# ScalarE's move of the transposed tile ahead of the slot's exponential, and three steps a third of a slot later

## The chip, the cores and the metric

The kernel runs on one core of a Trainium2 chip. The metric is the device time of one execution in microseconds. Engines are called PE (TensorE, matrix multiplication), DVE (VectorE), ACT (ScalarE), POOL (GpSimd) and SP (SyncE, which only issues DMAs here).

## What is computed

Eight sequences (B) of 512 rows (S) of 256 numbers (D) go through an adapter with a layer norm, and then through an attention block with a feed-forward part:

```python
# adapter: down to 64, exact gelu, one of 16 experts, up to 256, residual, layer norm
hidden = gelu(x @ down_W.T + down_b);  hidden = hidden @ Wsel.T + bsel + domain_emb
x = layernorm(hidden @ up_W.T + up_b + x) * ln_gamma + ln_beta
# attention block, 16 heads of 16
scale, shift = split(silu(sin_emb(timestep)) @ W_ada + b_ada)
x = ln(x) * (1 + scale) + shift
q, k, v = x @ Wq + bq, x @ Wk + bk, x @ Wv + bv
scores = q @ k.T / 4 + attention_bias;  scores[mask] = -inf      # (8, 16, 512, 512)
x = x + (softmax(scores) @ v) @ Wo + bo
h = ln(x) * g2 + beta2
out = x + gelu2(h @ W1 + b1) @ W2 + b2                            # gelu2(x) = x * sigmoid(1.702 x)
```

The attention bias is a tensor of its own for every head, 128 MB in all.

## The kernel before

The 4096 rows are cut into 16 chunks (`NCH`) of 256 rows. One iteration `i` of the main loop does the attention of chunk `i`: 16 heads times 2 blocks of 128 query rows are 32 slots (`TI`). The loop is unrolled into five instruction streams, one for each engine. Each engine works strictly in its own written order; semaphores alone tie them together.

In slot `t` of iteration `i` the engines do this for one tile of 128 queries by 512 keys:

- PE: `score(t)` (L805), one matmul of q and k, both split into bf16 parts, into bank `sc[t % 2]`. It waits for the maximum of slot t-2, which reads that bank.
- POOL: once for two slots, the mask is subtracted from the bias tile of a head (L489).
- DVE: `find_max(t)` (L1337) adds the bias to the scores, writes the sum over the bias tile and keeps a row value `mx`.
- ACT: `soften(t)` (L951), the exponential in place, with the row sums.
- PE: `turn(n)` (L812), four transposes of the exponentiated tile of four slots earlier (`LAG = 4`, `n = 32 i + t - 4`), into bank `tp[n % 2]`. It waits for exponential n and for the move of tile n-2.
- ACT or DVE: `move(n)` copies that bank to `pT` in SBUF. ACT has 21 of the 32 tiles (L957), DVE the 11 of `DVE_MOVES` (L1344), counted by tile. In the slots 12, 14, 15, 17, 19, 21, 24, 27 to 29 and 31, DVE moves.
- PE: `weigh` (L771), twice for each group of eight tiles, multiplies `pT` with the values.

So "move 9" below is the move that stands in slot 9, and "turn 11" the turn of slot 11.

Between these stand all the other steps: each has a time written out in a table, as slot plus 0, 0.3 or 0.6. `each_slot` runs the steps of `t.0`, then the first of two given actions, then the steps of `t.3`, the second action, and the steps of `t.6`. On PE the first is the score and the second the turn; on DVE the maximum and the move; on ACT, before, the exponential and the move. Within one time, the steps of the norm and of q, k, v come first, then the feed-forward's, then the output projection's.

The steps that matter here, for the chunk `a = i + 2` that is being prepared: the adapter's up matmul (PE 0.3), DVE's norms (1.6 to 10.6; the last, `shift`, writes `xm`, L1088), PE's `turn_rows` of xm at 12.6 (L555), ACT's copy of the result to `xT1` at 14.0 (L842), PE's `keys` (L581) at 15.3 and 16.0, which wait for this copy and for DVE's last part of q, and the splitting of k into three bf16 parts by turns: ACT 16.6, DVE 17.3, ACT 17.6, DVE 18.6, with the store by SP at 19.6. q of the next chunk is projected at 8.6 and 10.0 and split by ACT at 11.0 and 12.3 and by DVE at 11.6 and 13.0.

The feed-forward of chunk `i - 2` has eight up-projections `w1` (each a bias matmul L715 and two projections L717, of 128x256 outputs) in four pairs; each pair goes through ACT's `tanh` and DVE's `gate` (L1296), and a new pair waits until the gate has freed its bank. The eight `w2` steps (L734) are the down-projection. In odd iterations the next adapter down matmul runs at 24.3 and 25.3 and its gelu on ACT at 26.6, with a table load before and after it. The last three chunks have tables of their own in `ffn_at` and `mid_at`.

Of the kernel before, what the change touches and what calls it, by code (L numbers as in the profile page):

```python
# [29 lines left out]
LAG = 4  # L30
# [10 lines left out]

PE_AT = dict(up=0.3, v=(1.0, 2.0), q=(8.6, 10.0), xt1=12.6, k=(15.3, 16.0), down=(24.3, 25.3),
             pv=((14.0, 15.0), (22.0, 23.0), (30.0, 31.0), (6.0, 7.0)), spread=(23.3, 7.3))
ACT_AT = dict(q=(11.0, 12.3), widen=(18.3, 2.3), spread=(24.6, 8.0), k=(16.6, 17.6), xT1=14.0, gelu=26.6)
DVE_AT = dict(x1=1.6, st0=2.3, mv0=2.6, v=3.0, n1=4.0, n2=6.3, st1=7.0, mv1=7.6, m1=8.3, m2=10.6, q=(11.6, 13.0),
              k=(17.3, 18.6), recip=(17.6, 1.6), ctx=(25.3, 9.3))
SP_AT = dict(tail=1.0, x=3.0, q=13.6, stack=(17.0, 19.0, 26.0), mask=12.0, mod=12.3, xt=27.0, k=19.6,
             keys=(20.3, 22.0, 27.0))  # L50
POOL_AT = dict(rs0=6, rs1=8, xs=10, mask=16, rs2=16)
MID = dict(wo=(21.0, 21.6), x2=22.6, copy=23.0, st2=23.6, mv2=24.3, hn=27.0, ht=28.6)
FFN = dict(hT=30.0, w1=(3.0, 4.0, 8.0, 9.0, 12.3, 13.0, 17.0, 18.0), tanh=(5.0, 9.6, 14.3, 19.0),
           gate=(6.0, 10.3, 15.3, 19.6), w2=(19.0, 20.0, 23.6, 24.6, 25.6, 26.0, 27.0, 28.0), out=29.6, store=31.0)
GATE = 1.702 / 2
LAST = NCH
# [25 lines left out]
def ffn_at(f):  # L82

    at, i = dict(FFN, hT=FFN["hT"] - TI), f + 2
    if f == NCH - 3:
# [21 lines left out]
def wait(eng, sem, value):  # L107

    if value <= 0:
        return  # L110
    eng.wait_ge(sem, value)
# [7 lines left out]
def on_act(n):  # L119

    return n % TI not in DVE_MOVES
# [7 lines left out]
def head_of(hh):  # L129

    return 8 * (hh // 8) + 2 * (hh % GH) + hh // GH % 2
# [8 lines left out]
def each_slot(i, t, steps, first, second):  # L140

    steps(float(t), round(float(TI * i + t), 1))
    first()
    steps(round(t + 0.3, 1), round(TI * i + t + 0.3, 1))
    second()
    steps(round(t + 0.6, 1), round(TI * i + t + 0.6, 1))


def build(nc, x, x_t, t_tok, e_tok, bias, mask, downT, upT, up_b, experts, gamma, beta,
# [16 lines left out]
    with ExitStack() as ctx:  # L166
        def sb(name, shape, dt=F32):
            return ctx.enter_context(nc.sbuf_tensor(name, shape, dt))
# [42 lines left out]
        xT1 = [sb(f"xT1{n}", [P, CT, CH]) for n in range(2)]  # L211
# [20 lines left out]
        hT = sb("hT", [P, CT, CH])  # L232
# [318 lines left out]
        def _(pe):  # L551
# [117 lines left out]
            def body(i, attn, prev, nxt, pre, qv, down):  # L669
                a, c = i + 2, i + 1  # L670
                AT = PE_AT

# [158 lines left out]
        def _(act):  # L831
# [13 lines left out]
            def queries(c, part):  # L845
                if part == 0:
                    act.wait_ge(s["p_q"], c + 1)
                    wait(act, s["q_out"], 32 * c)
                    for mt in range(2):
                        cols = slice(mt * CH, (mt + 1) * CH)  # L850
                        last = act.activation(qb[:, 0, cols], q_bank(c)[:, cols], ACT.Identity, bias=nbq[:, mt:mt + 1])
                    last.then_inc(s["a_q0"], 1)
                else:
                    act.wait_ge(s["d_qr"], c + 1)
                    act.copy(qb[:, 1, :], q_bank(c)[:, :]).then_inc(s["a_q1"], 1)

            def keys(c, part):
                if part == 0:
                    act.wait_ge(s["p_k"], c + 1)
                    wait(act, s["k_out"], 64 * (c - 1))  # L860
                    for mt in range(2):
                        cols = slice(mt * CH, (mt + 1) * CH)
                        last = act.activation(kb[c % 2][:, 0, cols], k_bank(c)[:, cols], ACT.Identity,
                                              bias=vec[:, VEC["bk"] + mt:VEC["bk"] + mt + 1])
                    last.then_inc(s["a_k0"], 1)
                else:
                    act.wait_ge(s["d_kr"], c + 1)
                    act.copy(kb[c % 2][:, 1, :], k_bank(c)[:, :]).then_inc(s["a_k1"], 1)
# [20 lines left out]
            def body(i, attn, prev, nxt, pre, qv, down):  # L889
                a, c = i + 2, i + 1  # L890
                AT = ACT_AT

                def norm_steps(t):
                    if qv and t in AT["q"]:
                        queries(c, AT["q"].index(t))
                    if pre and t in AT["k"]:
                        keys(a, AT["k"].index(t))
                    if pre and t == AT["xT1"]:
                        copy_rows(a)
                    if down and t == AT["gelu"]:  # L900
                        adapter_gelu((i + 3) // 2)

                def ffn_steps(f, at):
                    when = ffn_at(f)
                    if at == when["hT"]:
                        act.wait_ge(s["p_ht"], f + 1)
                        wait(act, s["p_w1"], 4 * f)
                        for ct in range(CT):
                            last = act.activation(hT[:, ct, :], lb[:, ct * CH:(ct + 1) * CH], ACT.Identity,
                                                  scale=vec[:, VEC["g2"] + ct:VEC["g2"] + ct + 1],  # L910
                                                  bias=vec[:, VEC["beta2"] + ct:VEC["beta2"] + ct + 1])
                        last.then_inc(s["a_hT"], 1)
                    if at in when["tanh"]:
                        p = when["tanh"].index(at)
                        act.wait_ge(s["p_w1"], 4 * f + p + 1)
                        wait(act, s["d_act"], 4 * f + p - (1 if f == NCH - 1 else 0))
                        act.activation(tanh_of(f, p), w1_bank(f, p)[:, :], ACT.Tanh, scale=GATE  # L917
                                       ).then_inc(s["a_th"], 1)

                def mid_steps(m, at):  # L920
                    if at == mid_at(m)["copy"]:
                        act.wait_ge(s["d_x2"], m + 1)
                        wait(act, s["d_out"], m - 1)
                        act.copy(x2s[m % 2][:, :], lb[:, :]).then_inc(s["a_x2"], 1)

                def steps(t, at):
                    norm_steps(t)
                    for f in range(max(0, i - 2), min(i, NCH)):
                        ffn_steps(f, at)
                    if i > 0:  # L930
                        mid_steps(i - 1, at)
                    for r in range(2):
                        if (prev if r else attn) and t == AT["widen"][r]:
                            ri = 2 * (i - r) + r
                            act.wait_ge(s["d_recip"], ri + 1)
                            wait(act, s["p_rin"], ri)
                            act.copy(rwide[:, :, :].rearrange("p j (h d) -> p j h d", d=HD),
                                     rinv[:, :, :].unsqueeze(3).to_broadcast([P, 2, 8, HD])).then_inc(s["a_wide"], 1)
                        if (prev if r else attn) and t == (4.3 if i == NCH else AT["spread"][r]):
                            ri = 2 * (i - r) + r  # L940
                            act.wait_ge(s["p_rin"], ri + 1)
                            wait(act, s["d_ctx"], ri)
                            act.copy(rin[:, :], inverse_bank(ri)[:, CH:2 * CH]).then_inc(s["a_rin"], 1)

                def soften(t):
                    hh, j = t // 2, t % 2
                    act.wait_ge(s["smax"], TI * i + t + 1)
                    if t % (TI // 2) == 0:
                        wait(act, s["d_recip"], 2 * (i - 1) + t // (TI // 2) + 1)
                    tile = bias_s[:, (H * i + hh) % NB, j, :]  # L950
                    act.activation(tile, tile, ACT.Exp, bias=mx[:, t:t + 1], scale=-1.0,  # L951
                                   accum_out=sums[:, j, head_of(hh):head_of(hh) + 1]).then_inc(s["probs"], 1)

                def move(n):
                    act.wait_ge(s["pt_ready"], n + 1)
                    wait(act, s["pv_done"], n // TG - 1)
                    act.copy(pT[n // TG % 2][:, n // 2 % GH, :, (n % 2) * P:(n % 2 + 1) * P],  # L957
                             tp[n % 2][:, :].rearrange("p (k q) -> p k q", k=KT)).then_inc(s["copied_a"], 1)

                for t in range(TI):  # L960
                    n = TI * i + t - LAG
                    each_slot(i, t, steps, lambda: soften(t) if attn else None,
                              lambda: move(n) if (attn if t >= LAG else prev) and on_act(n) else None)

            each_iteration(body)

# [449 lines left out]
```

## Time and profile before

| | |
|---|---|
| median of 3 runs | 1038.88 us (1038.23 to 1039.96) |
| profiled execution | 1044.28 us, span 1042.4 us |
| granted clock of PE, mean of the span | 0.966 |
| busy, share of the span | PE 90%, DVE 69%, ACT 68%, POOL 66% |
| DMA | 207 MB, mean 199 GB/s |

The profile is of one execution. Busy time of PE counts matmuls whose ends are modelled and which overlap, so two matmuls may be shown over the same moment. In the timeline each line is an instruction, or several of one kind in a row (x4), with its start and duration in us, and in brackets how long the engine had been idle and what released it.

### The profile page before, as it was taken

To read this page: it belongs to the slowest core of one execution; us is meant where nothing else is said; L and a number is where in the kernel's file an instruction comes from. 1 tells how busy PE (TensorE), PEld (TensorE's weight loads), DVE (VectorE), ACT (ScalarE), POOL (GpSimd) and SP (SyncE) were. 2 spreads that over 40 slices of the span, in tenths; PEclk is the share of its full clock that TensorE was granted. 3 is DMA by queue.
4 is the path that set the end of the run, shared out by engine and by line. 5 is a ranking of instruction groups with operands and counts; after the bars stand their busy time and mean duration, and the time that the engine had idled before them with its cause. 6 is when DMAs were issued, how large, how long until landed. Compare 5 with 4: busy or idle time off the path is not lost.

```text
span 1042.4 us, 20949 instructions
## 1 busy us (share of the span) xinstructions
PE 935.6 (90%) x6621; PEld 663.3 (64%) x6621; DVE 720.7 (69%) x1911; ACT 707.6 (68%) x1675; POOL 685.7 (66%) x391
## 2 busy tenths in 40 slices
PE   3566888999999999999999999999999999999987
PEld 1444555676667766676667766676667767676665
DVE  5836766777777777777777777777777777674542
ACT  2225777777777777777777777777777777777541
POOL 2437786867677776867677676877677776784600
PEclk8678898999999999999999999999999999999998
DMA  5399758776796758765796659776796659665200
GB/s 159 91 263 296 240 187 234 222 212 192 227 275 181 212 182 245 220 212 193 225 275 184 209 182 236 228 213 193 218 261 187 196 178 264 206 199 151 90 11 11
DMA packets 147950, 207.42 MB, mean 199 GB/s; under 512 B 14385, under 2 KB 62322, under 8 KB 147842
## 3 DMA queue, kind: packets, MB, share of 16 engines
q1 hardware_dynamic: 147842, 206.09, 66.8%
q8 instruction: 55, 0.90, 0.4%
q14 instruction: 53, 0.43, 0.1%
HBM read 185.05 MB, written 20.99 MB: 198 GB/s over the span
## 4 chain that ended last, share of the span: by engine, by line
PE 51%; issue 16%; DVE 13%; ACT 11%; POOL 6%; DMA 1%; SPq 0%; DVEq 0%; ACTq 0%; POOLq 0%
PE tp L812 12%; PE pv L771 8%; PE la L734 7%; PE sc L805 6%; PE lc L717 6%; POOL bias_s L489 5%; DVE bias_s L1337 4%; PE lb L581 4%; ACT bias_s L951 3%; ACT pT L957 3%; PE lb L751 3%; DMA bias_s<-in_bias 1%; DVE st L1076 1%; DVE xm L1088 1%; PE lb L597 1%
## 5 line engine op out<-in xcount | busy, mean ns | idle before, releaser
L489 POOL TENSOR_TENSOR bias_s<-mask_f,bias_s 128x1024 f32<-128x1024 f32 x256 | 603.4, 2371 | 228.6 <-DMA bias_s<-in_bias 228.1
L951 ACT ACTIVATE bias_s<-bias_s,mx 128x512 f32<-128x512 f32 x512 | 369.9, 723 | 263.3 <-DVE mx L1337 259.4
L1337 DVE CUSTOM_DVE_ANT_0 bias_s<-sc,bias_s 128x512 f32<-128x512 f32 x512 | 348.5, 685 | 197.2 <-PE sc L805 182.6
L812 PE MATMUL tp<-ident,bias_s 128*128 128x128 f32 x2048 | 314.7, 277 | 41.9 <-ACT pT L957 38.4
L812 PEld LDWEIGHTS tp<-ident,bias_s 128*128 128x128 f32 x2048 | 251.6, 143 | 140.8 <-ACT bias_s L951 67.5
L805 PE MATMUL sc<-stk,stq 128*128 128x512 bf16 x512 | 198.0, 387 | 11.5 <-DVE mx L1337 9.4
L957 ACT COPY pT<-tp 128x512 f32<-128x512 f32 x336 | 191.1, 569 | 0.5 <-PE tp L812 0.5
L771 PE MATMUL pv<-pT,v_all 128*32 128x256 f32 x2048 | 138.7, 389 | 0.5 <-issue 0.5
L734 PE MATMUL la<-w_s,act_s 128*128 128x256 f32 x512 | 128.3, 380 | 1.0 <-DVE act_s L1296 1.0
L1344 DVE COPY pT<-tp 128x512 f32<-128x512 f32 x176 | 120.5, 685 | 7.9 <-PE tp L812 7.8
L717 PE MATMUL lc<-hT,w_s 128*128 128x256 f32 x464 | 122.0, 386 | 0.0
L805 PEld LDWEIGHTS sc<-stk,stq 128*128 128x128 bf16 x512 | 50.1, 98 | 74.5 <-DVE mx L1337 34.0
L951 ACT ACTIVATION_READ_ACCUMULATOR bias_s<-bias_s,mx 128x1 f32 x512 | 97.0, 190 | 0.0
L734 PEld LDWEIGHTS la<-w_s,act_s 128*128 128x128 f32 x512 | 89.2, 190 | 9.7 <-DVE act_s L1296 1.3
L717 PEld LDWEIGHTS lc<-hT,w_s 128*128 128x128 f32 x464 | 81.0, 195 | 9.5 <-issue 0.3
L771 PEld LDWEIGHTS pv<-pT,v_all 128*32 128x32 f32 x2048 | 54.1, 110 | 47.9 <-issue 25.8
L499 POOL TENSOR_SCALAR rs<-mv 128x2 f32<-128x2 f32 x48 | 9.3, 193 | 84.7 <-DVE mv L1083 82.5
L1296 DVE SCALAR_TENSOR_TENSOR act_s<-th,lc 128x512 f32<-128x512 f32 x57 | 39.2, 687 | 35.8 <-ACT th L917 35.7
L1337 DVE DVE_READ_ACCUMULATOR2_ANT mx<- 128x1 f32 x512 | 42.7, 83 | 0.0
L581 PE MATMUL lb<-xT,wk_s 128*128 128x256 f32 x120 | 34.0, 410 | 8.9 <-ACT xT L842 8.9
L715 PE MATMUL lc<-b1sel,b1p 128*128 128x256 bf16 x116 | 32.3, 278 | 7.7 <-DVE act_s L1296 4.3
L500 POOL TENSOR_TENSOR rs<-rs,powc 128x2 f32<-128x2 f32 x48 | 33.5, 698 | 4.0
(188 smaller groups left out, 848.4 us busy)
## 6 DMA issues: line engine op xcount, KB each, us to landing
bias_s<-in_bias SPq DMA_DIRECT2D x256, 512.0 KB, 4.2
stq<-q_parts SPq DMA_DIRECT2D x128, 96.0 KB, 3.7
stk<-k_parts SPq DMA_DIRECT2D x128, 96.0 KB, 4.0
k_parts<-kb SPq DMA_DIRECT2D x32, 192.0 KB, 2.3
q_parts<-qb SPq DMA_DIRECT2D x32, 192.0 KB, 2.3
xT<-in_x_t SPq DMA_DIRECT2D x8, 512.0 KB, 5.9
k_parts<-kb SPq DMA_DIRECT2D x32, 128.0 KB, 2.4
stq<-q_parts SPq DMA_DIRECT2D x64, 64.0 KB, 3.8
```

The source lines that it names most:

```text
L489: pool.tensor_tensor(tile, mask_f[:, :, :], tile, ALU.subtract).then_inc(s["masked"], 1)
L581: last = pe.matmul(bank[:, mt * CH:(mt + 1) * CH], w[:, ct, mt * P:(mt + 1) * P], xT1[c % 2][:, ct, :], start=(ct == 0), stop=(ct == CT - 1))
L717: last = pe.matmul(h, w1_s[:, ct, ft * P:(ft + 1) * P], hT[:, ct, :], start=False, stop=(ct == CT - 1))
L734: last = pe.matmul(rows, act_s[:, ft, j * P:(j + 1) * P], w2_s[:, ft, :], start=False, stop=(ft == FT - 1))
L771: last = pe.matmul(pv[32 * h:32 * h + 32, 0:CH], v[:, kt, col:col + 2 * HD], pT[gi % 2][:, h, kt, :], start=(g % 2 == 0 and kt == 0), stop ...
L805: pe.matmul(sc[t % 2][:, :].rearrange("p (e k) -> p e k", e=2), stq[:, hh, j * P:(j + 1) * P], stk[:, :, hh, :], start=True, stop=True).th ...
L812: last = pe.transpose(tp[n % 2][:, kt * P:(kt + 1) * P], bias_s[:, n // 2 % NB, n % 2, kt * P:(kt + 1) * P], ident[:, :])
L951: act.activation(tile, tile, ACT.Exp, bias=mx[:, t:t + 1], scale=-1.0, accum_out=sums[:, j, head_of(hh):head_of(hh) + 1]).then_inc(s["prob ...
L957: act.copy(pT[n // TG % 2][:, n // 2 % GH, :, (n % 2) * P:(n % 2 + 1) * P], tp[n % 2][:, :].rearrange("p (k q) -> p k q", k=KT)).then_inc( ...
L1296: dve.scalar_tensor_tensor(out=act_s[:, 2 * p:2 * p + 2, :].rearrange("p c n -> p (c n)"), in0=tanh_of(f, p), scalar=1.0, in1=w1_bank(f, p ...
L1337: dve.tensor_tensor_reduce(out=tile, in0=sc[t % 2][:, :], in1=tile, scale=1.0, scalar=BIG, op0=ALU.add, op1=ALU.min, accum_out=mx[:, t:t + ...
L1344: dve.tensor_copy(pT[n // TG % 2][:, n // 2 % GH, :, (n % 2) * P:(n % 2 + 1) * P], tp[n % 2][:, :].rearrange("p (k q) -> p k q", k=KT)).th ...
```

## The change

On ACT the move becomes the first action of a slot and the exponential the second. The two key projections go a third of a slot later on PE, ACT's two key parts from 16.6 and 17.6 to 17.0 and 18.0, DVE's first key part from 17.3 to 17.6. Four up-projections (the last two pairs) go a third of a slot or two thirds later. The feed-forwards of the last three chunks (13 to 15) have their own tables and keep them; chunks 0 to 12, in iterations 2 to 14, use the changed one.

```diff
-PE_AT = dict(up=0.3, v=(1.0, 2.0), q=(8.6, 10.0), xt1=12.6, k=(15.3, 16.0), down=(24.3, 25.3),
+PE_AT = dict(up=0.3, v=(1.0, 2.0), q=(8.6, 10.0), xt1=12.6, k=(15.6, 16.3), down=(24.3, 25.3),
...
-ACT_AT = dict(q=(11.0, 12.3), widen=(18.3, 2.3), spread=(24.6, 8.0), k=(16.6, 17.6), xT1=14.0, gelu=26.6)
+ACT_AT = dict(q=(11.0, 12.3), widen=(18.3, 2.3), spread=(24.6, 8.0), k=(17.0, 18.0), xT1=14.0, gelu=26.6)
...
-              k=(17.3, 18.6), recip=(17.6, 1.6), ctx=(25.3, 9.3))
+              k=(17.6, 18.6), recip=(17.6, 1.6), ctx=(25.3, 9.3))
...
-FFN = dict(hT=30.0, w1=(3.0, 4.0, 8.0, 9.0, 12.3, 13.0, 17.0, 18.0), tanh=(5.0, 9.6, 14.3, 19.0),
+FFN = dict(hT=30.0, w1=(3.0, 4.0, 8.0, 9.0, 13.0, 13.6, 17.6, 18.3), tanh=(5.0, 9.6, 14.3, 19.0),
...
-                    each_slot(i, t, steps, lambda: soften(t) if attn else None,
-                              lambda: move(n) if (attn if t >= LAG else prev) and on_act(n) else None)
+                    each_slot(i, t, steps, lambda: move(n) if (attn if t >= LAG else prev) and on_act(n) else None,
+                              lambda: soften(t) if attn else None)
```

## Rows read from the trace of the kernel before

**Rows 1.** The page, busy us, share of the span and instructions
```profile
PE 935.6 (90%) x6621; PEld 663.3 (64%) x6621; DVE 720.7 (69%) x1911; ACT 707.6 (68%) x1675; POOL 685.7 (66%) x391
```

**Rows 2.** Stretches: length; busy of PE, PEld, DVE, ACT, POOL; clock; DMA, GB/s
```profile
120.00:960.00 840.00, 796.31 (x5870) 570.35 (x5868) 611.37 (x1622) 628.93 (x1499) 610.01 (x339) 0.99 0.72 214
```

**Rows 3.** Waits of PE, 120 to 960 us: us in total, times, longest
```profile
PE tp L812 <- ACT pT L957: 29.9, 55, 1.3
PE lb L581 <- ACT xT L842: 7.1, 13, 1.0
```

**Rows 4.** Timeline of PE, iteration 8, slots 10 to 12: start, duration, [idle before]
```profile
552.43 0.38 PE L805 MATMUL sc<-stk,stq 128*128 128x512 bf16 x1
552.65 0.60 PE L812 MATMUL tp<-ident,bias_s 128*128 128x128 f32 x4
553.09 0.38 PE L805 MATMUL sc<-stk,stq 128*128 128x512 bf16 x1
553.63 0.63 PE L812 MATMUL tp<-ident,bias_s 128*128 128x128 f32 x4 [0.17 <-ACT pT L957]
554.10 0.38 PE L805 MATMUL sc<-stk,stq 128*128 128x512 bf16 x1
554.77 0.28 PE L715 MATMUL lc<-b1sel,b1p 128*128 128x256 bf16 x1 [0.29 <-DVE act_s L1296]
...
556.19 0.60 PE L555 MATMUL la<-ident,xm 128*128 128x128 f32 x4
```

**Rows 5.** Timeline of PE, iteration 8, slot 5
```profile
542.22 0.38 PE L805 MATMUL sc<-stk,stq 128*128 128x512 bf16 x1
543.24 0.63 PE L812 MATMUL tp<-ident,bias_s 128*128 128x128 f32 x4 [0.64 <-ACT pT L957]
```

**Rows 6.** Timeline of ACT, iteration 8, slot 9 and the tanh of 9.6
```profile
552.20 0.72 ACT L951 ACTIVATE bias_s<-bias_s,mx 128x512 f32<-128x512 f32 x1 [0.90 <-DVE mx L1337]
...
552.92 0.56 ACT L957 COPY pT<-tp 128x512 f32<-128x512 f32 x1
553.39 0.60 ACT L917 ACTIVATE th<-lc 128x512 f32<-128x512 f32 x1
```

**Rows 7.** Timeline, turns 20 and 31 of iteration 7, turn 0 of 8; exponential 27
```profile
511.36 0.63 PE L812 MATMUL tp<-ident,bias_s 128*128 128x128 f32 x4 [0.53 <-ACT pT L957]
...
531.01 0.73 ACT L951 ACTIVATE bias_s<-bias_s,mx 128x512 f32<-128x512 f32 x1
...
532.99 0.60 PE L812 MATMUL tp<-ident,bias_s 128*128 128x128 f32 x4
...
535.47 0.63 PE L812 MATMUL tp<-ident,bias_s 128*128 128x128 f32 x4 [0.80 <-ACT pT L957]
```

**Rows 8.** Timeline of PE, iteration 7, score 15 and the first keys
```profile
500.89 0.39 PE L805 MATMUL sc<-stk,stq 128*128 128x512 bf16 x1
501.79 1.13 PE L581 MATMUL lb<-xT,wk_s 128*128 128x256 f32 x4 [0.51 <-ACT xT L842]
```

**Rows 9.** Timeline of DVE, iteration 8: maximum 10, gate, xm, maximum 11
```profile
552.99 0.69 DVE L1337 CUSTOM_DVE_ANT_0 bias_s<-sc,bias_s 128x512 f32<-128x512 f32 x1 [0.48 <-PE sc L805]
...
554.02 0.69 DVE L1296 SCALAR_TENSOR_TENSOR act_s<-th,lc 128x512 f32<-128x512 f32 x1 [0.33 <-ACT th L917]
554.62 0.87 DVE L1088 SCALAR_TENSOR_TENSOR xm<-la,rs,mod 128x256 f32<-128x256 f32 x2
555.41 0.68 DVE L1337 CUSTOM_DVE_ANT_0 bias_s<-sc,bias_s 128x512 f32<-128x512 f32 x1
```

**Rows 10.** Waits of PE, 60 to 182 us (iterations 0 and 1)
```profile
PE tp L812 <- ACT pT L957: 15.1, 20, 1.3
...
PE tp L812 <- DVE pT L1344: 2.8, 2, 1.4
...
PE lb L581 <- ACT xT L842: 2.0, 2, 1.0
```

**Rows 11.** Stretches, 160 to 164 us (iteration 1)
```profile
160.00:164.00 4.00, 3.31 (x11) 2.60 (x12) 1.34 (x5) 2.54 (x7) 2.37 (x1) 0.50 0.76 217
```

## The prediction

> **What bounds the kernel now.** I read the page's busy times first, then the table of stretches, then the waits of TensorE (PE), and last the timelines of the slots in which it waits. The page gives PE 90% of the span. In the stretch 120 to 960 us it is busy for 796.3 of 840 us at a granted clock of 0.99, while VectorE (DVE), ScalarE (ACT) and GpSimd (POOL) each have 610 to 629 us [rows 1, 2]. So PE is the bound in the steady part, and what can be won is its own idle time, 43.7 us there. The waits name it: 29.9 us in 55 places before a `turn` (the four transposes of L812) until an ACT move has ended, and 7.1 us before the first key projection until ACT's copy of xT [rows 3]. The rest is mostly the wait for a gate at step 12.3, 0.29 us each time [rows 4]. In the timelines they come back at the same slots in each of the 12 iterations 2 to 13: slot 5 (0.64 us), slot 11 (0.17), slot 20 (0.53), step 15.3 (0.51), and at slot 0 (0.80) after each odd iteration, in which ACT also computes the adapter's gelu [rows 4, 5, 7, 8]. The 55 places are 12 at slot 5, 13 at slot 11, 12 at slot 20, 6 at slot 0, 10 in iteration 1 and 2 in iterations 14 and 15.
>
> **A wait costs more than its idle time.** In slot 10 nothing is waited for, and the turn starts 0.22 us after the score; in slot 11 there is 0.17 us of idle time, and it starts 0.54 us after: 0.32 late. In slot 5, with 0.64 idle, it starts 1.02 after: 0.80 late [rows 4, 5]. The score is shown busy for 0.38 us although its successor normally starts at 0.22, so each wait behind a score costs its idle time plus 0.16, and 0.03 more because the waiting group of four runs less overlapped (0.47 to its successor, against 0.44) [rows 4]. The Trainium skill's "Perfetto Trace Analysis" (section "Tensor Engine Instruction") says that the profiler estimates where a TensorE instruction ends and doesn't observe it; the spacing of starts here agrees. By idle times alone the steady part of the sum below would be 25 us, by starts it is 35, and I take the starts.
>
> **ACT's move ahead of its exponential.** Nothing is added or removed; two instructions of each slot trade places. Turn(t) overwrites the bank that the move of slot t-2 reads. In slot 9 ACT starts its exponential at 552.20, as late as that because it waited 0.90 us for DVE's maximum; the move runs from 552.92 to 553.48, and turn 11 starts at 553.63 [rows 4, 6]. The tile to be moved was there long before, since turn 9 stands a slot's work earlier on PE. Ahead of the exponential, move 9 ends near 552.3, while PE asks for turn 11 at 553.31. I walked the others in the same way: move 3 ends near 541.3 and PE asks at 542.44; move 18 ends 0.9 us before PE asks; move 30, queued behind gelu, three exponentials and the copy to hT, loses one exponential with its accumulator read (0.72, from 552.20 to 552.92) and about 0.3 from slot 26, where the move gets ahead too: it ends just before PE asks. So these waits go: slot 5 (0.64 + 0.19) and slot 20 (0.53 + 0.19) in 12 iterations, 18.6 us; slot 0, 0.99 in five iterations and 1.49 in iteration 2, 6.4 us [rows 5, 7].
> What is queued behind the move now is the exponential, which from here on waits for turn(t) as well as for the maximum. Turn(t+4) is the first to want its result, about 7 us later. The tightest place is the odd iteration, where exponential 27 stands behind gelu and two table loads: it starts at 531.01, is done at 531.74, and turn 31 starts at 532.99 [rows 7]. With 1.2 us left I cost this at nothing; if the cover were gone, it would be the overrun, in 7 iterations.
> ACT's steps at .3 stand between move and exponential as before, but on the other side of each. The tanh of 9.6 starts one move (0.47) earlier [rows 6]; q's second part at 12.3 gets ahead of exponential 12, so that the xT copy at 14.0 comes some 1 us earlier against PE.
>
> **Keys a third of a slot later.** The keys start 0.90 us after the score, 0.68 over the normal 0.22 [rows 8], and their group of four takes 0.09 longer than one without a wait: 0.77 in 12 iterations, 9.3 us, gone by the earlier copy alone; the later step only adds cover. On ACT, 16.6 to 17.0 and 17.6 to 18.0 change no place in the queue. On DVE, 17.3 to 17.6 lets the move of slot 17 go ahead of the keys' remainder; this ends the wait of turn 19 for that move, 1.4 us, in iterations 0 and 1 [rows 10]. SP's store of k at 19.6 follows DVE's part at 18.6, which doesn't move.
>
> **Up-projections: 12.3, 13.0, 17.0, 18.0 to 13.0, 13.6, 17.6, 18.3.** The first no longer waits for the gate of 10.3. But slots 10, 11 and 12 are now bare pairs of score and turn (0.66 us, from 552.43 to 553.09), and behind them at 12.6 comes `turn_rows`, which reads DVE's xm. Without a wait PE is there at 552.43 + 3 x 0.66 = 554.4 [rows 4]. On DVE, maximum 10 starts at 552.99 and frees the engine at 553.60 (its 0.69 less the overlap); the gate, now held by tanh until 554.02, follows at once and takes 0.60, and xm 0.87 more: it is there at 555.1, against 555.5 now [rows 9]. So PE waits 0.7 us at 12.6. The old delays were 0.32 + 0.03 at slot 11 and 0.67 - 0.22 = 0.45 at 12.3, the new one is 0.7: this part gives 0.1 us x 12 = 1 us, and the wait changes its name from gate to xm. The pair moved from 17.0 removes one wait, in iteration 14.
>
> **The ends.** Iterations 0 and 1 have no up-projections, so PE has less to do between its waits: from 60 to 182 us it waited 15.1 us for ACT moves, 2.8 for DVE moves and 2.0 for xT, in 24 places [rows 10]; with 0.19 each, 24.5 us. The largest, at slots 18 to 20, come from exponentials and key parts that stand ahead of moves, and go; but score 20 will then wait for maximum 18, which follows the key part. Bounds: 5 us (these three slots alone, half of it) to 24; I take 15, nearer to the upper since the order causes most of it. Iterations 14 and 15 hold 2 us behind turns and 0.8 behind gates: 2.5 us with the overlaps.
> Sum: 18.6 + 6.4 + 9.3 + 1 + 15 + 2.5 = 52.8 us. The profiled execution took 1044.3 us (span 1042.4) and would take 991.5; the median of the runs is 1038.9, 5.4 lower, and the same saving gives **986 us**. The period of an iteration, now 57.9 or 59.2 us, becomes about 55.6.
>
> **What else is near.** DVE, ACT and POOL, busy 73 to 75% now, go to 79% [rows 2]. The bias tiles' DMAs are issued when turns are done, so they come earlier with them.
>
> **Rivals.** (1) More: the clock falls less often, and xm comes in time. The stretch 160 to 164, right behind the three long waits of iteration 1, ran at 0.50, that is 1.2 GHz [rows 11]. PE's 3.3 us of work in it would take half at the other level; there are three such stretches from 100 us on, all in iterations 0 and 1, so 2 to 6 us, and xm in time 8 more: 972 to 980 us. The Trainium skill's "TensorE: Matmul & The Clock Gate" (section "Part 1: The HAM clock gate") says that lack of activity lowers the clock and activity frees it; the trace agrees, and the rule would add to the gain. Chance 0.15. (2) Half the waits come back under other names: scores that wait for maxima in the bare slots 10 to 12 and 16 to 20, and the ends giving 5: 24 to 34 us in all, 1005 to 1015 us. For it: maximum 11 starts at 555.41, 2.3 us after its score [rows 4, 9]. Against: PE shows no idle time for maxima in the steady part. Chance 0.17. (3) Slower: the ring of turn(t), move(t), exponential(t) and turn(t+4) becomes the pace, because each exponential now starts after a turn. It decides once an exponential lags its score by over four slots, 7 us; it outweighs the gain from 4.4 us per iteration on, and at 5 us gives 1046. Against: the largest lag now, behind gelu, is 4.4 us. Chance 0.04. (4) The change doesn't do what it says: the maximum and not the order holds the move, and all waits stay, 1038 us. Against: in slot 9 the order alone costs 0.72 us [rows 6]. Chance 0.02.
> My own case has 0.62 and reaches from 980 to 1000 us. Measurement can tell 0.2% from no change. Faster 0.94, within 0.2% 0.02, slower 0.04. The range, 974 to 1010, takes in most of rival 1 and half of rival 2.
>
> **What would show it.** Right: L812's idle time until ACT's pT in 120 to 960 us falls from 29.9 to under 5 us; the keys' wait for xT is gone; a new wait of L555 (la, xm) for DVE of about 0.5 us stands once in each of iterations 2 to 13; PE is busy 97% or more. Wrong: L805 waiting for the maximum, or L812 for ACT's exponential, by over 10 us; no wait at L555; a period above 57 us.

## The result

| | before | after |
|---|---|---|
| median of 6 runs | 1039.4 us (1038.2 to 1043.4) | 989.4 us (988.1 to 992.8) |
| profiled execution | 1044.3 us, span 1042.4 | 990.3 us, span 988.4 |
| ratio | | 0.952, 95% interval 0.950 to 0.954 |

The forecast was 986 us with a range from 974 to 1010: 50 us were saved where 52.8 were forecast. The page of the changed kernel: busy time, the chain that ended last, and from the groups of instructions the turn on PE and the move on ACT (busy us, mean ns | idle us before them, what ended it).

```profile
PE 918.3 (93%) x6621; PEld 663.4 (67%) x6621; DVE 715.2 (72%) x1911; ACT 708.5 (72%) x1675; POOL 685.4 (69%) x391
...
PE 80%; issue 7%; POOL 6%; DVE 5%; ACT 1%; DMA 1%; SPq 0%; POOLq 0%; DVEq 0%; ACTq 0%
...
L813 PE MATMUL tp<-ident,bias_s 128*128 128x128 f32 x2048 | 311.7, 275 | 8.1 <-ACT pT L958 4.9
...
L958 ACT COPY pT<-tp 128x512 f32<-128x512 f32 x336 | 195.9, 583 | 101.9 <-PE tp L813 99.5
```

The same work (6621 matmuls) is now 93% of the span, and the chain runs over PE for 80% of it. All lines have moved down by one. The move now waits 99.5 us for its turn: ACT stands ready in front of the tile instead of coming late to it. That idle time costs nothing. On the page of before the same move hardly ever waited (0.5 us in all):

```profile
L957 ACT COPY pT<-tp 128x512 f32<-128x512 f32 x336 | 191.1, 569 | 0.5 <-PE tp L812 0.5
```

The stretch that answers to [rows 2], and the waits of PE in it, which answer to [rows 3]:

```profile
120.00:910.00 790.00, 774.68 (x5797) 565.82 (x5797) 600.71 (x1607) 624.18 (x1485) 604.48 (x336) 1.00 0.76 224
```

```profile
PE sc L806 <- DVE mx L1338: 4.5, 3, 1.9
PE la L556 <- DVE xm L1089: 3.9, 12, 0.3
PE tp L813 <- ACT pT L958: 3.6, 7, 0.8
```

PE is busy 98% there, after 95%. The wait for ACT moves fell from 29.9 us in 55 places to 3.6 in 7, all of them in iterations 1 and 2; the keys' wait for xT is gone, and the new wait for xm stands exactly 12 times, once in each of iterations 2 to 13. The three long waits for a maximum are in iterations 1 and 2 as well. Here is the wait for xm in the timeline of PE, iteration 8, slots 10 to 13, with the same slots of iterations 9 and 10 behind it; this answers to [rows 4]:

```profile
518.53 0.38 PE L806 MATMUL sc<-stk,stq 128*128 128x512 bf16 x1
518.74 0.60 PE L813 MATMUL tp<-ident,bias_s 128*128 128x128 f32 x4
...
519.84 0.39 PE L806 MATMUL sc<-stk,stq 128*128 128x512 bf16 x1
520.27 0.63 PE L813 MATMUL tp<-ident,bias_s 128*128 128x128 f32 x4
521.22 0.66 PE L556 MATMUL la<-ident,xm 128*128 128x128 f32 x4 [0.33 <-DVE xm L1089]
...
522.69 0.38 PE L806 MATMUL sc<-stk,stq 128*128 128x512 bf16 x1
...
575.80 0.65 PE L556 MATMUL la<-ident,xm 128*128 128x128 f32 x4 [0.33 <-DVE xm L1089]
...
632.68 0.66 PE L556 MATMUL la<-ident,xm 128*128 128x128 f32 x4 [0.33 <-DVE xm L1089]
```

From one xm wait to the next are 54.58 and 56.88 us, 111.46 for two iterations. Before, turn 11 of iteration 8 started at 553.63 [rows 4] and that of iteration 10 at the line below, 117.15 us for two.

```profile
670.78 0.63 PE L812 MATMUL tp<-ident,bias_s 128*128 128x128 f32 x4 [0.17 <-ACT pT L957]
```

ACT in slot 9 and the tanh behind it, and DVE from maximum 10 to xm, in the changed kernel; they answer to [rows 6] and [rows 9]:

```profile
517.86 0.59 ACT L958 COPY pT<-tp 128x512 f32<-128x512 f32 x1 [0.60 <-PE tp L813]
518.34 0.72 ACT L952 ACTIVATE bias_s<-bias_s,mx 128x512 f32<-128x512 f32 x1
...
519.06 0.58 ACT L918 ACTIVATE th<-lc 128x512 f32<-128x512 f32 x1
519.54 0.59 ACT L958 COPY pT<-tp 128x512 f32<-128x512 f32 x1
```

```profile
519.08 0.69 DVE L1338 CUSTOM_DVE_ANT_0 bias_s<-sc,bias_s 128x512 f32<-128x512 f32 x1 [0.48 <-PE sc L806]
...
519.70 0.68 DVE L1297 SCALAR_TENSOR_TENSOR act_s<-th,lc 128x512 f32<-128x512 f32 x1
520.30 0.87 DVE L1089 SCALAR_TENSOR_TENSOR xm<-la,rs,mod 128x256 f32<-128x256 f32 x2
```

The move comes ahead of its exponential, the tanh follows both, and the gate no longer waits for the tanh: it starts at once behind the maximum (519.70), and xm is done 2.6 us after score 10 (518.53), where the forecast had 2.7. The next move, that of slot 10, stands behind the tanh and ends at 520.13; turn 12 starts 0.14 us later (520.27).

Last, the move that the prediction had left the least room, the one behind a gelu: move 30 and turn 0 in the timeline of iteration 8, which answers to [rows 7].

```profile
501.54 0.57 ACT L958 COPY pT<-tp 128x512 f32<-128x512 f32 x1
502.42 0.60 PE L813 MATMUL tp<-ident,bias_s 128*128 128x128 f32 x4
```

The move ends at 502.11, and turn 0 starts 0.31 later without a wait. Only turn 12 had less room, and it was held: it starts 0.43 us after its score, where 0.22 is normal.

**Where the 54 us between the two spans went.** I took the start of score 0 of each iteration from both timelines. Iterations 3 to 13, which repeat, are called the steady part from here on. Ahead of the loop 1.4 us were saved, in iteration 0 7.7 (63.7 to 56.0 us), in iteration 1 9.8 (57.9 to 48.1), in iterations 3 to 13 together 30.8, in iteration 14 1.3, and behind it 3.5. Iteration 2 took 0.5 us longer than before (58.4 to 58.9). That one was to save 3.9 us.

### The profile page after: what moved, and what is told of

It is laid out like the page before. It is cut to its first block, busy times and chain, and to the rows that moved or that the text cites. A ratio compares the mean times of both kernels' runs of the same rounds, so it can differ in the third digit from the quotient of the medians.

```text
span 988.4 us, 20949 instructions
## 1 busy us (share of the span) xinstructions
PE 918.3 (93%) x6621; PEld 663.4 (67%) x6621; DVE 715.2 (72%) x1911; ACT 708.5 (72%) x1675; POOL 685.4 (69%) x391
## 4 chain that ended last, share of the span: by engine, by line
PE 80%; issue 7%; POOL 6%; DVE 5%; ACT 1%; DMA 1%; SPq 0%; POOLq 0%; DVEq 0%; ACTq 0%
PE tp L813 19%; PE pv L772 12%; PE la L735 11%; PE sc L806 11%; PE lc L718 10%; POOL bias_s L490 5%; PE lb L582 4%; PE lb L752 3%; PE lb L598 2%; PE lc L716 1%; DVE xm L1089 1%; PE la L572 1%; PE lc L564 1%; PE la L556 1%; PE lb L556 1%
## 5 line engine op out<-in xcount | busy, mean ns | idle before, releaser
L490 POOL TENSOR_TENSOR bias_s<-mask_f,bias_s 128x1024 f32<-128x1024 f32 x256 | 603.1, 2373 | 188.4 <-DMA bias_s<-in_bias 188.1
L958 ACT COPY pT<-tp 128x512 f32<-128x512 f32 x336 | 195.9, 583 | 101.9 <-PE tp L813 99.5
L500 POOL TENSOR_SCALAR rs<-mv 128x2 f32<-128x2 f32 x48 | 9.3, 193 | 78.4 <-DVE mv L1084 76.0
L501 POOL TENSOR_TENSOR rs<-rs,powc 128x2 f32<-128x2 f32 x48 | 33.5, 699 | 4.0
L752 PE MATMUL lb<-wo_s,ctxn 128*128 128x256 f32 x128 | 33.0, 381 | 1.4 <-DVE ctxn L1318 1.4
```

What stands on the lines that cost most here:

```text
L490: pool.tensor_tensor(tile, mask_f[:, :, :], tile, ALU.subtract).then_inc(s["masked"], 1)
L752: last = pe.matmul(lb[:, j * D:(j + 1) * D], ctxn[:, ct, j * P:(j + 1) * P], wo_s[:, ct, :], start=(ct == 0), stop=(ct == CT - 1))
```

## Which part did it

Four kernels, each compared with the kernel before. First only the order on ACT, with the tables of before:

```diff
-                    each_slot(i, t, steps, lambda: soften(t) if attn else None,
-                              lambda: move(n) if (attn if t >= LAG else prev) and on_act(n) else None)
+                    each_slot(i, t, steps, lambda: move(n) if (attn if t >= LAG else prev) and on_act(n) else None,
+                              lambda: soften(t) if attn else None)
```

> Only ACT's order is changed; keys and up-projections keep the times of before. My theory (the order carries the gain; the later up-projections trade the wait for the gate at 12.3 for a slightly longer wait for xm at 12.6): 986 to 989 us, level with the changed kernel or up to 3 us below it. L805 to L812 waits for ACT moves gone as in the changed kernel, no wait at L555 for xm in iterations 2 to 13, a wait of 0.1 to 0.3 us at step 12.3 for the gate instead, no wait of the keys for xT, and turn 19 of iterations 0 and 1 waits about 1 us for DVE's move. Rival (the tables carry part of it): the wait of the keys stays, and with it 5 to 9 us: 995 us or more.

Measured: 985.7 us, ratio 0.948 (0.946 to 0.950). The order alone gives all that the change gives, and 0.4 us per iteration more: in iterations 3 to 13 it has periods (from one score 0 to the next) of 54.18 and 56.49 us by turns, the changed kernel 54.58 and 56.88. Its waits of PE, 120 to 910 us:

```profile
PE lc L716 <- DVE act_s L1297: 4.4, 15, 1.0
...
PE tp L813 <- DVE pT L1345: 2.1, 1, 2.1
```

The wait for the gate at 12.3 is still there, and turn 19's wait for the DVE move is 2.1 us, where I expected 1; it occurs in iterations 0 and 1 only. There the keys also still wait 0.36 us for xT, where I expected nothing; in the steady part they don't.

Then only the tables, with the exponential first and the move second as before (the changed entries alone, abridged from four lines):

```diff
-k=(15.3, 16.0)  k=(16.6, 17.6)  k=(17.3, 18.6)  w1=(..., 12.3, 13.0, 17.0, 18.0)
+k=(15.6, 16.3)  k=(17.0, 18.0)  k=(17.6, 18.6)  w1=(..., 13.0, 13.6, 17.6, 18.3)
```

> Only the tables are changed; ACT keeps the exponential first. My theory: the waits at slots 5, 20 and 0 stay in full, the keys' wait shrinks from 0.51 to about 0.2 us, and in slots 11 to 13 turn 12 now waits for move 10 and step 12.6 for xm, 0.4 us more than before: 1036 to 1041 us, no change that can be measured. Rival (the tables carry part of the gain): 1030 us or less.

Measured: 1025.3 us, ratio 0.986 (0.984 to 0.989). My theory was wrong and its rival right: the tables alone save 14 us. Its waits of PE (120 to 950 us) and turn 12 of iteration 7:

```profile
PE tp L813 <- ACT pT L958: 33.8, 57, 1.3
```

```profile
481.66 0.63 PE L813 MATMUL tp<-ident,bias_s 128*128 128x128 f32 x4 [0.83 <-ACT pT L958]
```

The waits at slots 5, 11 and 0 were there as expected, and turn 12's new wait as well (0.83 us of idle time, 12 times). But the keys' wait and the one at slot 20 were gone in all of iterations 2 to 13. Two more kernels ask which entry does it. The first has the keys' new times alone, the second those of the last up-projection pair alone, and the rest as before (the first edit is abridged from three lines):

```diff
-k=(15.3, 16.0)  k=(16.6, 17.6)  k=(17.3, 18.6)
+k=(15.6, 16.3)  k=(17.0, 18.0)  k=(17.6, 18.6)
 ...
```

> The kernel before with only the keys' times changed (PE 15.6 and 16.3, ACT 17.0 and 18.0, DVE 17.6). With the tables alone the kernel ran in 1025 us, where I expected no change; this and the next run ask which table entry does it. Theory: the keys. DVE's key part behind the move of slot 17 and keys behind turn 15 let maximum 18 start 1.3 us earlier, so move 18 is in time for turn 20 although the exponential stands ahead of it; and half of the keys' wait is covered. The waits at slots 5, 11, 12.3 and 0 stay as before, the period falls from 57.9 and 59.2 to about 56.8 and 58.1 us, and iterations 0 and 1 lose the wait of turn 19: 1018 to 1026 us. Rival (the up-projections from 17.0 and 18.0 do it): 1033 us or more, with the wait at slot 20 as before.

```diff
-w1=(3.0, 4.0, 8.0, 9.0, 12.3, 13.0, 17.0, 18.0)
+w1=(3.0, 4.0, 8.0, 9.0, 12.3, 13.0, 17.6, 18.3)
 ...
```

> The kernel before with only the last pair of up-projections moved, from 17.0 and 18.0 to 17.6 and 18.3. Theory of the keys: score 18 is 1 us earlier, but maximum 18 stands behind DVE's key part, which waits for ACT, so nothing changes at slot 20: 1036 to 1041 us. Rival: the wait of 0.53 us at slot 20 goes and the time is 1030 us or less.

Measured: the keys' times alone 1022.4 us, ratio 0.985 (0.980 to 0.989), period 56.91 and 58.24; the pair alone 1038.1 us, ratio 0.999 (0.996 to 1.001). Waits of PE, first with the keys' times (120 to 945 us), then with the pair (120 to 960 us):

```profile
PE tp L812 <- ACT pT L957: 23.5, 45, 1.3
```

```profile
PE tp L812 <- ACT pT L957: 30.0, 56, 1.3
PE lb L581 <- ACT xT L842: 7.1, 13, 1.0
```

With the keys' times the 12 waits at slot 20 and the keys' own are gone; with the pair both are as in [rows 3]. The keys' table works through DVE. Its first key part waits for ACT, and behind it stand the move of slot 17 and maximum 18. In the timeline of iteration 7 with the keys' times (PE, then DVE, then DVE) score 18, the key part and maximum 18:

```profile
492.18 0.38 PE L805 MATMUL sc<-stk,stq 128*128 128x512 bf16 x1
```

```profile
492.32 0.88 DVE L1164 SCALAR_TENSOR_TENSOR lb<-lb,vec,kb 128x256 f32<-128x256 f32 x2
...
493.26 0.63 DVE L1337 CUSTOM_DVE_ANT_0 bias_s<-sc,bias_s 128x512 f32<-128x512 f32 x1
```

and with the pair alone:

```profile
502.81 0.38 PE L805 MATMUL sc<-stk,stq 128*128 128x512 bf16 x1
...
503.88 0.88 DVE L1164 SCALAR_TENSOR_TENSOR lb<-lb,vec,kb 128x256 f32<-128x256 f32 x2 [1.44 <-ACT kb L863]
...
505.43 0.63 DVE L1337 CUSTOM_DVE_ANT_0 bias_s<-sc,bias_s 128x512 f32<-128x512 f32 x1
```

Maximum 18 starts 1.1 us after its score in the first, 2.6 us in the second. In the kernel before, DVE's key part had waited less:

```profile
507.41 0.88 DVE L1164 SCALAR_TENSOR_TENSOR lb<-lb,vec,kb 128x256 f32<-128x256 f32 x2 [0.47 <-ACT kb L863]
```

The pair brought score 18 forward by a microsecond, and the key part's wait for ACT, which grew from 0.47 to 1.44 us, used it up: counted from score 0, maximum 18 starts at 34.8 us with and without the pair, and at 33.8 with the keys' times. So the wait at slot 20 and the keys' wait each have two cures, the order and the keys' times. Either is enough; together they do not add. The later up-projections cost something besides (3 us between the tables alone and the keys' times alone, 5 us in the next section), so the parts' savings, 53 and 14, come to 50 in the change and not to 67.

## What each table entry is worth once the order is changed

The changed kernel with the up-projections back:

```diff
-w1=(3.0, 4.0, 8.0, 9.0, 13.0, 13.6, 17.6, 18.3)
+w1=(3.0, 4.0, 8.0, 9.0, 12.3, 13.0, 17.0, 18.0)
```

> The changed kernel with the up-projections back at 12.3, 13.0, 17.0 and 18.0. My theory: they are worth less than nothing once the order is changed, since step 12.3 fills the time in which step 12.6 would wait for xm: 984 to 988 us, the period of iterations 3 to 13 shorter by 0.2 to 0.5 us, no wait at L555. Rival (the later up-projections are worth their place): 991 us or more, with a wait at 12.3 longer than the 0.33 us of idle time at L555.

Measured: 984.4 us, ratio 0.947 (0.945 to 0.948), iterations 3 to 13 at 54.18 and 56.49 us, no wait at L556, and 0.21 us for the gate at step 12.3 in each of them. The later up-projections lose 0.4 us per iteration, 5 us in all.

The changed kernel with the keys back:

```diff
-k=(15.6, 16.3)  k=(17.0, 18.0)  k=(17.6, 18.6)
+k=(15.3, 16.0)  k=(16.6, 17.6)  k=(17.3, 18.6)
```

> The changed kernel with the keys back at the times of before. Theory: with the move first, the keys' times matter only in iterations 0 and 1, where turn 19 then waits about 2.1 us for DVE's move of slot 17, as it does with the order alone: iterations 3 to 13 keep 54.6 and 56.9 us, 990 to 994 us. Rival (the keys' times hold part of the steady gain as well): their period grows by 0.5 us or more, 996 us or above.

Measured: 992.3 us, ratio 0.956 (0.951 to 0.960); iterations 3 to 13 unchanged (54.58 and 56.88), and in iterations 0 and 1 turn 19 waits 2.11 us each time. The waits of PE have it once, since their stretch starts at 120 us with iteration 1:

```profile
PE tp L813 <- DVE pT L1345: 3.0, 2, 2.1
```

The 3 us between this kernel and the changed one are not clear of the noise: it ran twice, and its interval overlaps the other's. What is shown is that the keys' times are worth nothing in the steady part once the order is changed.

The two steps at 12.6 and 13.0 changed round:

```diff
-xt1=12.6, ...  w1=(3.0, 4.0, 8.0, 9.0, 13.0, 13.6, 17.6, 18.3)
+xt1=13.0, ...  w1=(3.0, 4.0, 8.0, 9.0, 12.6, 13.6, 17.6, 18.3)
```

> The changed kernel with PE's turn_rows at 13.0 instead of 12.6 and the fifth up-projection at 12.6 instead of 13.0, so that these two trade places. If the 0.33 us of idle time at L555 is a wait for xm that other work can fill: the wait goes, 0.5 us in each of 12 iterations, 982 to 985 us. Rival (it only comes back at the next step, as a wait for the gate or a maximum): 988 to 991 us with the same idle time under another name.

Measured: 983.5 us, ratio 0.946 (0.944 to 0.948), 6 us less than the changed kernel. The period is 54.03 and 56.33, 0.55 shorter, and PE is busy for 605.4 of the 605.8 us of iterations 3 to 13. The xm wait was one that other work can fill.

## Is the exponential off the path

One more instruction on ACT right behind each exponential, in both orders, to a tile that nobody reads (four spare tiles of 128x128 in turn, and a semaphore of their own for the reuse), so that the computation is unchanged:

```diff
                     act.activation(tile, tile, ACT.Exp, bias=mx[:, t:t + 1], scale=-1.0, ...)
+                    wait(act, s["spared"], TI * i + t - 3)
+                    act.copy(spare[t % 4][:, :], ident[:, :]).then_inc(s["spared"], 1)
```

> The kernel before with one more ACT instruction right behind each exponential, a copy of 128x128 into a tile that nobody reads, 0.2 to 0.3 us. Theory (with the exponential first, it lies on the way from the maximum to the move and from there to PE's turn): each wait for a move grows by the copy or more, 1 us or more per iteration, 1052 to 1065 us, and L812's idle time until ACT's pT grows by 10 us or more. Rival (ACT has 30% idle time, so its length doesn't count): under 1043 us.

> The changed kernel with the same extra copy behind each exponential, now behind the move as well. Theory (the exponential has four slots of room): only where several exponentials or the tanh stand in a row does it show, at turn 12 (0.2 us) and at turn 0 after a gelu (0.5 to 0.8 us): 992 to 999 us, less than half of what the same copy adds to the kernel before. Rival (ACT as a whole became the pace once PE is at 98%): it adds as much as before or more, 1003 us or above, with PE waiting for ACT in most slots.

Measured: 1074.4 us with the old order, 35 more; 998.6 us with the new one, 9 more. The two kernels that got the copy differ in the tables too; the copy was not tried on the order alone. PE's waits with the old order (120 to 985 us), then with the new one (120 to 910 us):

```profile
PE tp L813 <- ACT pT L960: 47.4, 60, 2.1
PE lb L582 <- ACT xT L843: 13.5, 13, 1.2
```

```profile
PE tp L814 <- ACT pT L961: 10.1, 24, 1.7
PE la L557 <- DVE xm L1092: 3.8, 12, 0.3
```

The same copy costs almost four times as much where the exponential stands ahead of the move. With the new order the added waits stand at turn 12 (0.2 to 0.3 us of idle time) and at turn 0 after a gelu (0.45 us), as expected, and cost 0.2 to 0.9 us per iteration. With the old one it cost more than I expected (1052 to 1065): 1.3 to 2.3 us per iteration, and in addition the granted clock of PE fell to half three times in the steady part, in iterations 6, 8 and 12, for 5 us together. A stretch of 4 us around one of these, in iteration 6:

```profile
428.00:432.00 4.00, 3.19 (x13) 2.48 (x14) 0.26 (x1) 2.96 (x10) 3.48 (x2) 0.67 1.08 323
```

There the engine had just waited 1.78 us for a move at slot 0, and so it had before the other two. Iterations with such a fall took 61.9 us, the like ones without it 60.2.

## Why iteration 2 gained nothing

In the changed kernel, iteration 2, the timeline has this (POOL's masks L490 and rsqrt L500, L501; DVE's normalize L1089; maximum 7; score 9 on PE):

```profile
170.47 4.72 POOL L490 TENSOR_TENSOR bias_s<-mask_f,bias_s 128x1024 f32<-128x1024 f32 x2 [4.48 <-DMA bias_s<-in_bias]
...
175.58 2.36 POOL L490 TENSOR_TENSOR bias_s<-mask_f,bias_s 128x1024 f32<-128x1024 f32 x1 [0.38 <-DMA bias_s<-in_bias]
...
178.29 0.69 POOL L501 TENSOR_TENSOR rs<-rs,powc 128x2 f32<-128x2 f32 x1
...
179.02 0.88 DVE L1089 SCALAR_TENSOR_TENSOR la<-la,rs,beta_r 128x256 f32<-128x256 f32 x2 [3.95 <-POOL rs L501]
...
180.62 0.67 DVE L1338 CUSTOM_DVE_ANT_0 bias_s<-sc,bias_s 128x512 f32<-128x512 f32 x1
...
181.36 0.39 PE L806 MATMUL sc<-stk,stq 128*128 128x512 bf16 x1 [1.87 <-DVE mx L1338]
```

A bias tile lands 4.5 us after POOL asks for it; POOL's rsqrt for the norm stands behind three masks; DVE waits 3.95 us for it with maximum 7 queued behind; PE waits. The DMA engines were busy all of that stretch (share 1.06 from 162 to 178 us), with the keys' loads for the next sequence among the bias tiles. A bias tile took 10.7 us from issue to landing there (median, 158 to 178 us), against 4.3 in the whole kernel and 6.8 in the like stretch of the kernel before (176 to 197 us). My explanation is that iteration 1 was 10 us shorter and its DMAs no longer had that time. Three kernels move an rsqrt ahead of a mask. The first:

```diff
-POOL_AT = dict(rs0=6, rs1=8, xs=10, mask=16, rs2=16)
+POOL_AT = dict(rs0=5, rs1=8, xs=10, mask=16, rs2=16)
```

> The changed kernel with POOL's first rsqrt (L500, L501) one head earlier in POOL's queue, ahead of the mask of head 5 instead of behind it. My theory for iteration 2, which didn't get shorter: its masks wait for bias tiles (DMA share 1.06 in that stretch), the rsqrt stands behind them, DVE's normalize waits 4 us for it, and score 9 waits 1.9 us for maximum 7. So with the rsqrt ahead, score 9's wait goes and iteration 2 takes 56 to 57 us instead of 58.9; the rest stays: 986 to 988 us, and iterations 3 to 13 keep 54.6 and 56.9 us. Rival (the bias tile itself is late, and the rsqrt only looks like the cause): iteration 2 stays at 58.9 us and the time at 988 to 990 us, with DVE waiting for POOL's mask instead.

Measured: 990.9 us, ratio 0.954 (0.949 to 0.958), no change against the changed kernel, where I expected 986 to 988. Score 9's wait was gone as expected, but iteration 2 took 57.7 us, not 56 to 57, and this came in its place on PE:

```profile
188.22 0.66 PE L556 MATMUL la<-ident,xm 128*128 128x128 f32 x4 [1.99 <-DVE xm L1089]
```

xm needs the second rsqrt, and that one stands behind masks as well. In iteration 1 the same wait came (1.95 us), where the changed kernel has none. Together with the two steps changed round:

```diff
-xt1=12.6, ...  w1=(..., 13.0, 13.6, 17.6, 18.3)  rs0=6
+xt1=13.0, ...  w1=(..., 12.6, 13.6, 17.6, 18.3)  rs0=5
```

> Both edits that helped or should help: turn_rows at 13.0 with the fifth up-projection at 12.6, and POOL's first rsqrt one head earlier. If the two causes are apart, the gains add: 980 to 982 us. If the rsqrt is not the cause of iteration 2, it stays at 983 to 984 us.

Measured: 983.3 us, ratio 0.946 (0.941 to 0.950): nothing from the first rsqrt. With both rsqrts one head earlier:

```diff
-xt1=12.6, ...  w1=(..., 13.0, 13.6, 17.6, 18.3)  rs0=6, rs1=8
+xt1=13.0, ...  w1=(..., 12.6, 13.6, 17.6, 18.3)  rs0=5, rs1=7
```

> turn_rows at 13.0 with the fifth up-projection at 12.6, and both of POOL's rsqrts one head earlier. With only the first one earlier, score 9's wait in iteration 2 went and a wait of 2.0 us for xm came, since xm needs the second rsqrt, which stands behind masks too. Theory: with both ahead, iteration 2 takes about 56.5 us instead of 57.1 to 58.9, the other iterations stay at 54.0 and 56.3: 981 to 983 us. Rival (then the masks themselves are late, because the DMAs are): iteration 2 stays above 57.5 us.

Measured: **979.0 us**, ratio 0.943 (0.939 to 0.947), the fastest of all. That is better than the expected 981 to 983. Iteration 2 takes 55.2 us and has one wait of PE left, 1.0 us at slot 0; the others stay at 54.03 and 56.34. Iteration 0 gained as well (54.6 to 53.0 us): the longest wait of PE behind the start, that of score 9 for maximum 7 in iteration 0 (7.2 us in the changed kernel, 8.0 with the two steps changed round), fell to 4.4. PE's stretch:

```profile
120.00:910.00 790.00, 781.59 (x5866) 573.63 (x5859) 605.63 (x1619) 628.19 (x1494) 610.70 (x342) 1.00 0.77 225
```

So the late rsqrts were the cause in iteration 2, with late bias tiles ahead of them. That the tiles were late because iteration 1 got shorter was not tried. The traces fit it as far as they go: in the three kernels with the old order and no extra copy that were made for this study, and in the kernel before, iterations 0 and 1 take 112 to 122 us together and iteration 2 is 0.5 us longer than later even ones; in the six with the new order and POOL's queue unchanged they take 104 to 108 us, and iteration 2 is 3.1 to 4.4 us longer.

## The forecast, point by point

- **The bound, and what can be won.** Right. PE's idle time from 120 us on fell from 5% to 2%, and its 55 waits for moves to 7.
- **A wait costs more than its idle time.** Right: iterations 3 to 13 were to save 31.4 us by the starts (35.3 without iteration 2's 3.9) and saved 30.8; by idle times it would have been about 22.
- **Move ahead of exponential.** Right at slots 5, 11, 20 and 0, and right that the exponential has room. The order alone, and the copy behind each exponential, show it. One move was overlooked: move 10, behind the tanh, which still holds turn 12 by 0.21 us. It changed nothing in the sum, since xm comes later still.
- **Keys a third of a slot later.** The sum was right, since the order ends the keys' wait by itself. The step "the later step only adds cover" was wrong taken by itself: the keys' times are worth 17 us in the kernel before. I had followed DVE's key part only to the move of slot 17, and not on to maximum 18 and move 18, although both are queued behind it. The forecast for the whole was saved by the overlap of the two cures.
- **Up-projections.** Right in mechanism and size: gate's wait away, xm's in its place. By the timeline, turn 12 is 0.21 late (520.27, where 0.22 after score 12 was normal) and L556 0.51 late (0.95 after turn 12, for 0.44): 0.72 for the 0.7 forecast. The saving in these slots was then 0.1 at most, and the kernel with the old times, 0.4 faster per iteration, shows that the edit lost.
- **Iteration 2.** Wrong: 3.9 us forecast, minus 0.5 measured. I treated it like the other eleven. The failing step was "The bias tiles' DMAs are issued when turns are done, so they come earlier with them", with no term in the sum for it: bias tiles took 10.7 us to land where iteration 2 starts, and two rsqrts stand behind masks in POOL's queue.
- **The ends.** Iterations 0 and 1: 15 us forecast, 17.5 measured between the profiles. Score 20 waits for maximum 18 there, as forecast (1.28 us each time). Part of the gain is rival 1's clock: in iteration 1 PE's waits fell by 4.8 us and its busy time by 5.0 us, and the granted clock rose from 0.91 to 1.00, as the stretches of iteration 1 before and after show:

  ```profile
  123.58:181.48 57.90, 48.30 (x342) 30.39 (x340) 39.86 (x110) 41.36 (x97) 42.45 (x24) 0.91 0.74 222
  ```

  ```profile
  114.55:162.63 48.08, 43.28 (x343) 28.23 (x341) 39.68 (x110) 40.46 (x96) 41.83 (x25) 1.00 0.81 246
  ```

  These two iterations vary between the kernels of this study: iteration 1 took 47.3 to 51.6 us in those with the new order, and so the totals of two kernels can differ by 3 us without a cause in the steady part. The profiled execution of before was a slow one of its kind: the kernel with the pair alone, whose time is the same, took 118.1 us for them and not 121.6, and against it 14.0 us were saved. Iterations 14, 15 and the tail: 2.5 forecast, 4.8 measured.
- **The sum.** That 52.8 came so near 54.0 is in part luck: iteration 2 gave 4.4 us less than forecast, the ends 4.8 more, and 1.4 us were saved ahead of the loop, for which the sum had no term. The steady part alone was forecast to 0.6 us.
- **From profile to median.** The profiled execution of before was 4.9 us above its median, that of after 0.9. The saving between profiles was 54.0 us, between medians 50.0; the forecast sum of 52.8 was between the two.
- **Rivals.** Fuller gain (1): the clock part came, xm did not come in time. Waits under another name (2): xm's, and score 20's in iterations 0 and 1, both named in the prediction, and iteration 2's, which was not. Slower (3) and no effect (4): refuted by the time; the copy behind the exponential shows why (3) is far off.

## What to carry to other kernels

On an in-order engine, put first what the bound engine waits for soonest, and last what has slots of room, even where both come ready at the same moment: here that trade was worth 5% with no instruction changed. When a queue entry moves, follow everything behind it to the next engine and back, to the end; two edits may cure the same wait, and then their gains do not add. When a bare stretch appears on the bound engine, put work there whose inputs are oldest; and once the steady part is full, look for small steps, like an rsqrt, that stand behind DMA-fed work in a third engine's queue.

## What was not expected of the hardware

- A single wait can be followed by a lower clock in the middle of a well-filled kernel: with the extra copy and the old order the granted clock fell to 0.50 (1.2 GHz) three times in iterations 3 to 13, each time right behind the wait of 1.8 us at slot 0, and each such iteration took 1.7 us longer (61.9 beside 60.2). It does not always follow: in iterations 4 and 10 PE waited as long at the same place and the clock stayed at 1.00. With the new order, and with the old one without the copy (longest wait 0.8 us there), it never fell in these iterations. The Trainium skill's "TensorE: Matmul & The Clock Gate" (section "A second HAM failure mode: psum-queue depth-cycling") tells of a clock that oscillates where PE idles shortly and often between groups of matmuls; here the falls stand behind one longer wait, so the trace does not show that pattern.
- The steady part repeats to 0.01 us from iteration to iteration and from kernel to kernel (54.58 us in the changed kernel and in two of the others), so a profile alone tells apart edits worth 0.1 us per iteration, while the runs' medians move by 3 us with the first two iterations.
